# A graph-network kernel on one core: the sums of the last segment move to GpSimd, and one masked raise takes the place of two

## The reference, cut to what matters

```
seg_sum = segment_sum(edge_attr, src, N)
seg_max = where(cnt > 0, segment_max(edge_attr, src, N), 0)
seg_mean = seg_sum / max(cnt, 1)
h = concatenate([seg_sum, seg_max, seg_mean, u[batch]], axis=1)      # 97 columns
out = x + relu(h @ W1 + b1) @ W2 + b2
```

## Time and profile before

| | |
|---|---|
| device time, median of 3 runs | 4303.77 us (4302.16 to 4304.75) |
| profiled execution | 4299.8 us, its span 4298.0 us |
| mean granted TensorE clock | 0.669 |
| busy share: PE, DVE, ACT, POOL | 69%, 69%, 33%, 72% |
| tail, from the landing of the last segment's first load | 4128.35 to 4298.0 us |

### The profile page before, as it was taken

The page is one execution under the profiler, slowest core; times in us unless marked ns, Lnnn a source line. Parts: engine busy times, 40 slices in busy tenths (PEclk is TensorE's granted clock), DMA queues, the critical chain, the costliest instruction groups (busy, mean ns, idle before and its releaser), DMA issues.

```text
span 4298.0 us, 87474 instructions
## 1 busy us (share of the span) xinstructions
PE 2953.8 (69%) x18710; PEld 2191.8 (51%) x18710; DVE 2986.4 (69%) x12043; ACT 1418.7 (33%) x4649; POOL 3084.1 (72%) x3143
## 2 busy tenths in 40 slices
PE   5677667776666666666666677777787777767747
PEld 3455446654444444444444466666665556546635
DVE  6478559974555455554455589988897888769976
ACT  3333332243333333333333323332233333322224
POOL 5777777777777777777777777776677777777620
PEclk9977558765555555555555578877776788668867
DMA  7899863311111111111111333333322333134333
GB/s 295 333 378 377 333 243 114 115 25 25 26 26 26 26 25 26 26 26 26 25 26 26 82 103 101 106 108 103 100 65 78 91 88 92 52 90 120 88 111 103
DMA packets 410044, 454.47 MB, mean 106 GB/s; under 512 B 65002, under 2 KB 381460, under 8 KB 409620
## 3 DMA queue, kind: packets, MB, share of 16 engines
q1 hardware_dynamic: 309876, 401.37, 28.4%
q0 software_dynamic: 100000, 51.40, 4.9%
HBM read 221.50 MB, written 231.02 MB: 105 GB/s over the span
## 4 chain that ended last, share of the span: by engine, by line
POOL 41%; issue 21%; DVE 20%; PE 7%; DMA 6%; POOLq 2%; DVEq 1%; ACT 1%; SPq 0%; ACTq 0%
POOL sorted_rows L439 41%; DVE peak_ps L799 5%; DMA sorted_rows<-edges,position 3%; DVE raised L782 3%; DVE picked L723 3%; PE misc_ps L526 3%; DMA edges<-in_edge_attr 2%; DVE lent L715 2%; PE start_ps L495 1%; DVE hot_owner L706 1%; POOLq L439 1%; DVE rank_c L733 1%; DVE peak_ps L777 1%; PE same_ps L472 1%; DVE raised L810 1%
## 5 line engine op out<-in xcount | busy, mean ns | idle before, releaser
L439 POOL DMA_INDIRECT sorted_rows<-edges,position x3125 | 3075.2, 984 | 1035.5 <-issue 927.7
L499 PE MATMUL place_ps<-start_sb,lent 98*128 98x128 bf16 x3125 | 877.7, 281 | 1019.2 <-DVE rank_f L723 1017.6
L610 ACT ACTIVATE start_sb<-start_ps 98x128 bf16<-98x128 f32 x3125 | 867.6, 278 | 1660.1 <-PE start_ps L495 806.0
L495 PE MATMUL start_ps<-hot_owner,hot_block 128*98 128x128 bf16 x3125 | 980.1, 314 | 143.9 <-ACT start_sb L610 105.5
L723 DVE CUSTOM_DVE_ANT_0 picked<-place_ps,hot_owner 128x128 bf16<-128x128 f32 x3125 | 886.2, 284 | 102.0 <-issue 61.5
L499 PEld LDWEIGHTS place_ps<-start_sb,lent 98*128 98x128 bf16 x3125 | 377.6, 121 | 1131.2 <-DVE rank_f L723 1100.1
L501 PE MATMUL place_ps<-hot_owner,lent 128*128 128x128 bf16 x3125 | 894.8, 286 | 0.0
L738 DVE SCALAR_TENSOR_TENSOR position<-rank_c,src_f 128x5 int32<-128x5 f32 x625 | 104.4, 167 | 1057.2 <-DMA sorted_rows<-edges,position 1007.2
L495 PEld LDWEIGHTS start_ps<-hot_owner,hot_block 128*98 128x98 bf16 x3125 | 460.6, 147 | 625.6 <-ACT start_sb L610 614.6
L472 PE MATMUL same_ps<-lent 98*128 98x128 bf16 x3125 | 654.2, 288 | 74.9 <-DVE lent L715 35.3
L526 PE MATMUL misc_ps<-win,ident_f 128*128 128x224 f32 x2548 | 699.6, 437 | 0.0
(11 more groups left out here) (79 smaller groups left out, 1402.3 us busy)
## 6 DMA issues: line engine op xcount, KB each, us to landing
sorted_rows<-zeros SPq DMA_DIRECT2D x110, 1568.0 KB, 17.1
win<-sorted_rows SPq DMA_DIRECT2D x56, 1344.0 KB
edges<-in_edge_attr SPq DMA_DIRECT2D x625, 80.0 KB
sorted_rows<-edges,position POOLq DMA_INDIRECT x3125
win<-sorted_rows SPq DMA_DIRECT2D x28, 1008.0 KB
win<-sorted_rows SPq DMA_DIRECT2D x14, 1680.0 KB
win<-sorted_rows SPq DMA_DIRECT2D x14, 1568.0 KB
win<-sorted_rows SPq DMA_DIRECT2D x14, 896.0 KB
```

What stands on the lines that cost most here:

```text
L439: nc.gpsimd.indirect_dma_start(out=rows[:, :], out_offset=bass.IndirectOffsetOnAxis(ap=position[:, t:t + 1], axis=0), in_=edges[:, k, j * ...
L495: nc.tensor.matmul(start_ps[0:BLOCKS, 0:P], hot_block[:, t, :], hot_owner[:, t, :], start=False, stop=False, skip_group_check=True).then_i ...
L499: nc.tensor.matmul(place_slot(j), hot_block_t[:, slot, j * P:(j + 1) * P], start_sb[:, j, :], start=True, stop=False)
L610: nc.scalar.activation(start_sb[:, j, :], start_ps[0:BLOCKS, 0:P], ACT.Copy)\
```

## The change

The pair sum leaves VectorE. GpSimd, whose queue has nothing behind the last scatter, adds ranks 0 to 5 and 6 to 11 of `win` into `paired` and then, in a second operation that waits for the first, ranks 3 to 5 of `paired` to ranks 0 to 2. PE sums three ranks in place of six. SP loads the next half into `win` only when GpSimd's first addition has been done too. VectorE makes one mask of 12 ranks, in a place of `peak_ps` for each half, and one raise of 2688 columns.

```diff
-    last_steps = 4 + len(levels(depth[LAST]))
+    last_steps = 2 + len(levels(depth[LAST]))
+    QUARTER_LAST = HALF_LAST // 2
+        last_masks = [peak_ps[:, h * 128:h * 128 + depth[LAST] * SLOTS] for h in range(2)]
...
                     if f < 2:
                         sp.wait_ge(unit_summed, p * 2 + (f % 2 + 1))
+                    else:
+                        sp.sem_inc(pass_seen, 1)
+                        sp.wait_ge(pairs_added, q * HALVES + (f - 1))
                     load_half(LAST, f, 0, f % 2)
...
+                for f in range(HALVES):
+                    h = f % 2
+                    p = q * PAIRS + (pair_base[LAST] + f // 2)
+                    pool.wait_ge(win_loaded[h], p * 16 + 16)
+                    pool.wait_ge(unit_summed, p * 2 + (h + 1))
+                    nc.gpsimd.tensor_tensor(paired[:, h, :, :], win[:, h, 0:HALF_LAST, :],
+                                            win[:, h, HALF_LAST:2 * HALF_LAST, :], ALU.add).then_inc(pairs_added, 1)
+                    pool.wait_ge(pairs_added, q * HALVES + (f + 1))
+                    nc.gpsimd.tensor_tensor(paired[:, h, 0:QUARTER_LAST, :], paired[:, h, 0:QUARTER_LAST, :],
+                                            paired[:, h, QUARTER_LAST:HALF_LAST, :], ALU.add).then_inc(pairs_halved, 1)
...
                 def sum_last(f):
-                    pe.wait_ge(pairs_added, q * HALVES + (f + 1))
+                    pe.wait_ge(pairs_halved, q * HALVES + (f + 1))
-                    for r in range(HALF_LAST):
+                    for r in range(QUARTER_LAST):
...
-                    left, done = depth[LAST], 3
+                    left, done = depth[LAST], 1
...
+                    mask = last_masks[h].rearrange("p (r b) -> p r b", b=SLOTS)
+                    nc.vector.tensor_tensor(mask, left_t[:, f * SLOTS:(f + 1) * SLOTS].unsqueeze(1)
+                                            .to_broadcast([P, depth[LAST], SLOTS]),
+                                            iota_f[:, 0:depth[LAST]].unsqueeze(2).to_broadcast([P, depth[LAST], SLOTS]),
+                                            ALU.is_le).then_inc(unit_step, 1)
+                    dve.wait_ge(unit_step, steps + 1)
                     dve.wait_ge(win_loaded[h], p * 16 + 16)
-                    if f >= 2:
-                        dve.wait_ge(unit_summed, p * 2 + (h + 1))
-                    nc.vector.tensor_tensor(paired[:, h, :, :], win[:, h, 0:HALF_LAST, :],
-                                            win[:, h, HALF_LAST:2 * HALF_LAST, :], ALU.add).then_inc(pairs_added, 1)
-                    raise_half(LAST, h, f * SLOTS, 0, steps)
+                    nc.vector.scalar_tensor_tensor(
+                        raised[:, h, 0:depth[LAST], :].rearrange("p r (b f) -> p r b f", f=FEAT),
+                        mask.unsqueeze(3).to_broadcast([P, depth[LAST], SLOTS, FEAT]), -FLT_MAX,
+                        win[:, h, 0:depth[LAST], :].rearrange("p r (b f) -> p r b f", f=FEAT), ALU.mult, ALU.add)\
+                        .then_inc(win_raised, 1)
                     dve.wait_ge(win_raised, p * 2 + (h + 3))
                     take_max(h, f * SLOTS, steps)
```

More of the change, by code:

```diff
@@ L88, in build @@
     assert HALF_LAST * 2 == depth[LAST]
+    QUARTER_LAST = HALF_LAST // 2
+    assert QUARTER_LAST * 2 == HALF_LAST
     src_view = src.rearrange("(p t) -> p t", p=P)
@@ L212, in build @@
         pairs_added = sem("pairs_added")
+        pairs_halved = sem("pairs_halved")
         unit_summed = sem("unit_summed")
@@ L549, in sum_last @@
                     h = f % 2
-                    pe.wait_ge(pairs_added, q * HALVES + (f + 1))
+                    pe.wait_ge(pairs_halved, q * HALVES + (f + 1))
                     pe.wait_ge(sum_folded, q * (PAIRS * 2) + (pair_base[LAST] * 2 + f + 1))
-                    for r in range(HALF_LAST):
+                    for r in range(QUARTER_LAST):
                         last = nc.tensor.matmul(last_sums[h], ident_f[:, :], paired[:, h, r, :], start=(r == 0),
-                                                stop=(r == HALF_LAST - 1))
+                                                stop=(r == QUARTER_LAST - 1))
                     last.then_inc(unit_summed, 1)
```

## The result

The changed kernel takes 4328.73 us (median of 4 runs, 4323.85 to 4331.6) against 4303.73, a ratio of 1.0056 with a 95% interval from 1.0042 to 1.0069: 25 us slower. The forecast was 4323 and slower, in the range. Its profiled execution took 4323.85 us with a span of 4322.1, 24.1 above the span before. But those 24.1 us don't all lie where I put them: 12.8 came ahead of the tail and 11.3 in it.

The account below looks back on a forecast made before the run. VectorE was taken to bound the tail, PE and ScalarE close behind. +17.4 (first five halves) + 7.5 (next eight) - 1.9 (half 13) - 1.1 (end) = +21.9: 4321.7 us profiled, forecast 4323, range 4291 to 4338.

Parts of the forecast that it names:

- the tail: Everything from the last segment's first load at 4128.35 us on, 169.7 us of the span; forecast 21.9 us longer.
- The port: In SBUF, VectorE operations with two SBUF inputs and GpSimd's adds exclude each other, 3.9 us a half; PSUM-input operations are free.
- A: GpSimd's first add of a half, 1344 columns, estimated at 3.0 us.
- B: GpSimd's second add of a half, 672 columns, estimated at 1.5 us.
- The first five halves: Start of the last segment: halves 0, 2 and 4 drawn out by GpSimd's adds, 1 and 3 undisturbed; +17.4 us.
- The next eight: Halves 5 to 12: four pairs, each a 7.75 us half and a long one, 89.6 us against 82.1; +7.5 us.
- The last half and the end: Half 13 takes 6.9 us for 8.8, -1.9; PE's last sum falls to half, -1.1 us.
- The change touches nothing of that: GpSimd's scatters and what feeds them, ahead of the last segment, were taken as untouched; nothing in the sum.
- VectorE keeping the port over its row of operations: Rival: GpSimd's adds run only beside raise, fold and add_out; some 8.7 us a half, 4294 us; chance 0.17.
- No conflict: Rival: GpSimd's adds and VectorE's operations don't shut each other out in the last segment; 4284 us; chance 0.13.
- GpSimd was not quicker: Rival: GpSimd's adds take two thirds of the estimate, the first 2.0 to 2.2 us; 4302 us; chance 0.12.
- Everything in a row: Rival: none of GpSimd's adds overlaps with VectorE in the last segment; +31, less 1, 4334 us; chance 0.13.

Follow-up runs that it names:

- adds left out: The changed kernel with GpSimd's two adds removed, its queue only passing signals and PE summing three ranks of zeros: 4282.5 us, ratio 0.9961, tail 151.3 us.
- timed add: The changed kernel with GpSimd's first add waiting for its half's mask and the second add gone, PE summing six ranks: 4289.9 us, ratio 0.998, tail 153.8 us.

## Why the prediction came out, point by point

**The port: right, and shown.** Which operations are shut out, and which not, came out as listed (adds left out, timed add). So did the durations: A 3.0 (3.01 to 3.04 unhindered), B 1.5 (1.62), the raise 2.96, the mask 0.25. The rule of the Trainium skill (SBUF — State Buffer, "SBUF: two separate sides"), that whoever starts first keeps the port for its whole instruction, is now borne out by GpSimd's long adds as well: the mask at 4197.89, begun 0.1 us after one, takes 3.02 us in place of 0.25 and ends with it. The estimate from the Trainium skill's GPSIMD Engine Reference, section 3.1, was 2.95 and 1.5 us for the adds; the trace has 3.02 and 1.62.

**The first five halves: right in kind, a little too large.** The maximum of half 0 and the disturbed second and fourth came as worked out; the raise of half 5 starts 59.7 us after that of half 0, so the half itself at 59.4, against 45.6 before: +13.8, not +17.4. From raise to raise half 0 takes 16.3, half 2 14.7 and half 4 14.1 us, where I had 17.4, 15.5 and 16.0.

**The next eight: mis-sized.** They take 81.7 us (to the mask at 4282.34), so -0.4 against 82.1 where I put +7.5. The step that failed is "From there a pair is 7.75 and a long half": four times the 22.4 - 15.5 us that two pairs of adds would cost VectorE in a long half, 27.6 in all. The trace has 16.5: the maxima are 14.2 us longer than eight times 3.3, the mask of half 8 is 2.3 longer; VectorE's waits for PE, for which I had added nothing, are 2.2. I let GpSimd run a load ahead all the time. The rows show it waiting for PE four times, 17.4 us: `paired[h]` is free only when PE has summed half f - 2, and that sum stands behind the network of older halves in PE's queue. I had the wait in the diff and priced it at nothing. What it does fits the rows: each half gets one pair of adds, which starts nearer to the raise; six of the eight lose 1.5 to 3.0 us in the maximum, half 8 loses 2.3 in the mask. That this wait set the pattern is argued from these rows; no run took it away.

**The last half and the end:** -1.9 came as forecast, -1.1 came as -0.2 (from the last but one fold to the end of the span 32.8 us, 33.1 before). The tail: +13.8 - 0.4 - 1.9 - 0.2 = +11.3, for +21.9.

**"The change touches nothing of that": wrong.** This sentence about the scatters failed. The diff touches no scatter, but the last one came 12.8 us later in the profiled execution, and three kernels that have nothing else changed are 0.3% slower. That the total was met as closely as it was is luck, from two errors of opposite sign: the tail forecast 10.6 us too long, and 12.8 us that were not in the sum.

**The rivals.** VectorE keeping the port over its row of operations falls: GpSimd got in between the steps of the maximum, as the 8.59 us of half 0 show. No conflict falls as well; without adds the tail would be 18.3 us shorter, near the 17 worked out for it. GpSimd was not quicker. Everything in a row (+30 in the tail) is far from the +11.3 measured there. And the masks, which I had worth 0.4 us a half, show in VectorE's rows when they stand alone, but not in the length of the tail.

What stays open: why a tensor_tensor or a tensor_copy in GpSimd's program makes each scatter 5 ns longer. The runs tell the kind of operation from its place, its number and the length of the queue; they don't tell the mechanism, and iota and affine select were not tried apart.

## What to carry to other kernels

In this kernel an elementwise sum on an idle GpSimd was nearly free beside a VectorE operation with an input in PSUM: tie its start to such an operation (2.5 us over 14 halves) and don't let it start when its data happen to land (17 us more for the same sum). Before giving GpSimd a new kind of work, look at what it does all the time: one operation of 8 columns made 3125 scatters slower and cost 0.3% of the kernel, where the well-timed sums and the one raise had won some 0.5. And an engine that is granted only part of its clock, as PE here, may do extra sums for less than their count says.

## What the runs showed of the hardware

With a tensor_tensor or a tensor_copy anywhere in GpSimd's program an indirect DMA on GpSimd takes 977 or 978 ns at the median (seven kernels), without one 972 (five kernels), some 0.3% of this kernel's time over its 3125 scatters. I had not expected that. PE was granted 0.93 of its clock in a stretch in which it had more to do (busy 78 of 80 us), against 0.79 in the same stretch of the kernel before (67 of 82).
